# Self-attention of a decoder layer: the four key tiles' probabilities added on GpSimd, one product with ones per step

## Chip, cores and metric

The kernel runs on one core of a Trainium2 chip. The time is device microseconds of that core for one execution; three runs of the kernel before gave 2581.31 us as their median (2580.84 to 2584.7).

## What is computed

One decoder layer for B = 4 sequences of T = 512 rows with H = 512 features, in float32: a gated recurrence, a cross-attention over 1601 context rows, a causal self-attention with 16 heads of 32, and a mixture of experts with a shared expert. The change lies in the self-attention alone:

```python
q = (h @ wq + bq).reshape(B, S, N_HEADS, HEAD_DIM)   # k, v alike
q, k = _rope(q, k)
scores = jnp.einsum('bqhd,bkhd->bhqk', q, k) * HEAD_DIM ** (-0.5)
scores = jnp.where(causal[None, None], scores, jnp.finfo(scores.dtype).min)
attn = jax.nn.softmax(scores, axis=-1)
ctx = jnp.einsum('bhqk,bkhd->bqhd', attn, v).reshape(B, S, N_HEADS * HEAD_DIM)
x = x + ctx @ wo
```

## The kernel before

Four stages follow each other, each in a block of its own with a barrier behind it. Self-attention (`self_attention`) is the third and takes 16 **steps** (`STEPS`): step n works on sequence b = n // 4 and on the group c = n % 4 of four heads (`HPC` = 4). In a step the keys go by in four tiles of 128 rows, kt = 0 to 3. Because of the causal mask tile kt meets only the L = 512, 384, 256 or 128 queries behind it.

For a tile, TensorE (PE) computes the scores of the four heads into four PSUM banks (`scores`, L1727, the masks in L1731 and L1733); ScalarE (ACT) takes their exponential from all four banks in one instruction (L1529) into `pT`, a tile with two halves that alternate by kt; and `weighted` multiplies the probabilities by the values (L1745, into `o_bank`) and by a matrix of ones (L1747, into `sum_bank`). The second product gives the denominators of the softmax. The four heads of a product lie in four column groups of 32 of the array, so they run beside each other.

The maximum that softmax subtracts is made one step ahead. Between the scores of step n and those of its next key tile, PE writes plain scores for step n+1 into the *same four banks* (`maxima`, L1717 and L1719), and VectorE (DVE) reduces them (L1616) before PE may write the next scores there. At the end of a step PE transposes the four maxima (item T, L1711), ACT negates them (L1501), and they enter the next step's scores as one more product. Then DVE forms 1/sum from `sum_bank` (`reciprocal`, L1648), multiplies `o_bank` by it (L1650) and, with ACT (L1507), splits the result into a high and a low part (L1620) for the output projection.

PE's order is written out by hand in class `Steps`. A tile runs: scores(n, kt); the *early* items; maxima(n+1, 3-kt); weighted(n, kt); the *late* items. Items are the projections of later steps (A: queries and keys of step n+2; V: values; O: output projection of the sequence before; each 12 matmuls in L134), transposes of the next sequence's input (H, late in tiles 1 and 2 of c = 1, for b < 3), and in steps 14 and 15 the start of the experts (G, R, L). Step 1 has no item in tile 3, step 2 none in tiles 2 and 3, step 13 none in tile 2.

GpSimd (POOL) makes the rotary part of the queries and keys of step n+2 while step n runs: `rotate` (L1427 multiplies by cos, L1430 adds the part that DVE has turned in L1581 and multiplied by sin in L1583), then the high parts (L1444) and low parts (L1447), which wait until the scores of step n are done because the buffers alternate. It also makes inverse roots of four numbers (`inverse_root`, L1420), for H when c = 0 and for O when c = 3.

Of the kernel before, what the change touches and what calls it, by code (L numbers as in the profile page):

```python
# [20 lines left out]
P = 128  # L21
# [1301 lines left out]
def self_attention(nc, X, regions, first, ahead, hx, slots, ident, ident16, d):  # L1323
# [6 lines left out]
    with ExitStack() as stack:  # L1330
# [12 lines left out]
        qk = m.sb("qk", [P, 2, T])  # L1343
        turned = m.sb("turned", [P, 2, T])
        rot = m.sb("rot", [P, 2, T])
        pT = A.tile("s_pT", 0, 2, HPC, T)
        a_hi, a_lo = (A.tile(f"s_a{i}", (2 * HPC + i * RING) * T, RING, T, dt=F32R) for i in range(2))
        xs = A.tile("s_xs", (2 * HPC + 2 * RING) * T, TT, H)
        wo_raw = pT[:, 0]
        a = m.sb("a", [P, T])  # L1350
        topx = m.sb("topx", [P, TT, P])
        negm = m.sb("negm", [P, T], F32R)
# [4 lines left out]
        ss = m.sb("ss", [P, TT])  # L1357
        ms = m.sb("ms", [P, TT])
        rr = m.sb("rr", [P, TT])
        unused = pT[:, 1, :, T - P:T]  # L1360
        psum, bank = m.banks()
        s_apart = m.sem("apart")
        s_bank, o_bank, sum_bank = bank[0:HPC], bank[4], bank[5]
# [4 lines left out]
        s_whi, s_wlo = m.sem("whi", "wlo")  # L1368
        s_ss, s_ms, s_r, s_xs, s_put, s_hhi, s_hlo = m.sem("ss", "ms", "r", "xs", "put", "hhi", "hlo")
        s_vs, s_qb, s_tc, s_turned, s_sin, s_rot, s_hi, s_lo = m.sem("vs", "qb", "tc", "turned", "sin", "rot", "hi", "lo")  # L1370
        s_max, s_top, s_ng, s_st, s_ex, s_pv = m.sem("max", "top", "ng", "st", "ex", "pv")
        s_rec, s_a, s_ahi, s_alo, s_x1, s_x = m.sem("rec", "a", "ahi", "alo", "x1", "x")
        s_in, s_ahead, s_wrhi, s_wr = m.sem("in0", "in1"), m.sem("ahead"), m.sem("wrhi"), m.sem("wr")
        s_ghi, s_glo, s_lt, s_lc = m.sem("ghi", "glo", "lt", "lc")
# [32 lines left out]
        @block.gpsimd  # L1407
        def _(pool):
            pool.memset(half[:], -0.5).then_inc(s_const, 1)
            pool.memset(neg[:], 0.0).then_inc(s_const, 1)  # L1410
            pool.wait_ge(s_const, 2)
            pool.affine_select(out=neg[:], in_=neg[:], compare_op=ALU.is_ge, fill=-1e30, base=0,
                               pattern=[[-1, P]], channel_multiplier=1).then_inc(s_const, 1)

            def inverse_root(kind, b):
                u = line.root(kind, b)
                pool.wait_ge(s_ms, u + 1)
                if u:
                    pool.wait_ge(s_xs, u * TT)
                pool.tensor_tensor(rr[:], ms[:], half[:], ALU.pow).then_inc(s_r, 1)  # L1420

            def rotate(n, i):
                r = 2 * (n - 1) + i
                pool.wait_ge(s_qb, r + 1)
                if r >= 2:
                    pool.wait_ge(s_lo, r - 1)
                pool.tensor_tensor(rot[:, i], qk[:, i], cos[:], ALU.mult).then_inc(s_tc, 1)  # L1427
                pool.wait_ge(s_tc, r + 1)
                pool.wait_ge(s_sin, r + 1)
                pool.tensor_tensor(rot[:, i], rot[:, i], turned[:, i], ALU.add).then_inc(s_rot, 1)  # L1430

            pool.wait_ge(s_ld, 80)
            for n in range(1, STEPS):
                for i in range(2):
                    rotate(n, i)
                if n % KC == 2 and n // KC + 1 < B:
                    inverse_root("H", n // KC + 1)
                if n % KC == 1 and n // KC >= 2:
                    inverse_root("O", n // KC - 2)
                if n >= 2:  # L1440
                    pool.wait_ge(s_st, KC * (n - 1))
                for i in range(2):
                    pool.wait_ge(s_rot, 2 * (n - 1) + i + 1)
                    pool.tensor_copy(qk_hi[:, n % 2, i], rot[:, i]).then_inc(s_hi, 1)  # L1444
                for i in range(2):
                    pool.wait_ge(s_hi, 2 * (n - 1) + i + 1)
                    pool.tensor_tensor(qk_lo[:, n % 2, i], rot[:, i], qk_hi[:, n % 2, i], ALU.subtract).then_inc(s_lo, 1)  # L1447
            for b in (B - 2, B - 1):
                inverse_root("O", b)

        @block.scalar
        def _(act):
# [64 lines left out]
            for n in range(STEPS):  # L1517
                b, c = divmod(n, KC)
                if n == STEPS - 2:
                    act.wait_ge(s_ahead, 64)  # L1520
                    act.activation(wr_hi, wr, ACT.Copy).then_inc(s_wrhi, 1)
                for kt in range(TT):
                    L = T - kt * P
                    act.wait_ge(s_st, n * KC + kt + 1)
                    if n * TT + kt >= 2:
                        act.wait_ge(s_pv, n * TT + kt - 1)
                    else:
                        act.wait_ge(s_wlo, 1)
                    act.activation(pT[:, kt % 2, :, 0:L], psum[:, 0:HPC, 0:L], ACT.Exp, scale=SCALE).then_inc(s_ex, 1)  # L1529
                    if c == 1 and kt < 2 and b + 1 < B:  # L1530
                        normalise("H", b + 1, (2 * kt, 2 * kt + 1))
                    for item in line.early[n][kt]:
                        take(item)
                    if kt == 0 and n:
                        high_output(n - 1)
                    for item in line.late[n][kt]:
                        take(item)
                    if c == 0 and kt < 2 and b + 1 < B:
                        squares("H", b + 1, (2 * kt, 2 * kt + 1))
                    if c == 2 and kt == 0 and b:  # L1540
                        squares("O", b - 1, (0, 1))
                    if c == 3 and kt == 0 and b:
                        squares("O", b - 1, (2, 3))
                    if c == 3 and kt >= 2 and b:
                        normalise("O", b - 1, (2 * kt - 4, 2 * kt - 3))
                if n + 1 < STEPS:
                    take(line.turn[n + 1])
# [9 lines left out]
        def _(dve):  # L1557
# [71 lines left out]
            for n in range(STEPS):  # L1629
                b, c = divmod(n, KC)  # L1630
                if n == STEPS - 2:
                    dve.wait_ge(s_wrhi, 1)
                    dve.tensor_tensor(wr_lo, wr, wr_hi, ALU.subtract).then_inc(s_wr, 1)
                for kt in range(TT):
                    if n + 1 < STEPS:
                        maximum(n + 1, TT - 1 - kt)
                    if kt == 0 and n:
                        low_output(n - 1)
                    for item in line.early[n][kt] + line.late[n][kt]:
                        take(item)  # L1640
                    if c == 0 and kt == 2 and b + 1 < B:
                        mean("H", b + 1)
                    if c == 3 and kt == 0 and b:
                        mean("O", b - 1)
                dve.wait_ge(s_pv, n * TT + TT)
                if n:
                    dve.wait_ge(s_alo, n)
                dve.reciprocal(a[:], sum_bank).then_inc(s_rec, 1)  # L1648
                dve.wait_ge(s_rec, n + 1)
                dve.tensor_tensor(a[:], o_bank, a[:], ALU.mult).then_inc(s_a, 1)  # L1650
# [8 lines left out]
        def _(pe):  # L1659
# [76 lines left out]
            def weighted(n, kt):  # L1736
                c, L, qs = n % KC, T - kt * P, slice(kt * P, T)
                pe.wait_ge(s_ex, n * TT + kt + 1)
                if kt == 0 and n:
                    pe.wait_ge(s_a, n)  # L1740
                if n % KC == 0:
                    pe.wait_ge(s_vs, n // KC * TT + kt + 1)
                for j in range(HPC):
                    hd = c * HPC + j
                    pe.matmul(o_bank[rows[j], qs], v[:, kt, hd * SD:(hd + 1) * SD], pT[:, kt % 2, j, 0:L], start=kt == 0, stop=True, skip_group_check=True)  # L1745
                for j in range(HPC):
                    mm = pe.matmul(sum_bank[rows[j], qs], ones[:], pT[:, kt % 2, j, 0:L], start=kt == 0, stop=True, skip_group_check=True)  # L1747
                mm.then_inc(s_pv, 1)

            for t in reversed(range(TT)):  # L1750
                if t < TT - 1:
# [4 lines left out]
            for n in range(STEPS):  # L1756
                more = n + 1 < STEPS
                for kt in range(TT):
                    if kt == 0:
                        if n:  # L1760
                            pe.wait_ge(s_lo, 2 * n)
                    elif more:
                        pe.wait_ge(s_top, (n + 1) * TT + kt)
                    else:
                        pe.wait_ge(s_ex, n * TT + kt)
                    scores(n, kt)
                    for item in line.early[n][kt]:
                        put(item)
                    if more:
                        if kt == 0:  # L1770
                            pe.wait_ge(s_hi, 2 * n + 2)
                        pe.wait_ge(s_ex, n * TT + kt + 1)
                        maxima(n + 1, TT - 1 - kt)
                    weighted(n, kt)
                    for item in line.late[n][kt]:
                        put(item)
                if more:
                    put(line.turn[n + 1])
            for item in line.ahead + line.last + line.between + line.behind + line.end:
# [717 lines left out]
```

## Time and profile before

| | |
|---|---|
| runs of the kernel before, median | 2581.31 us |
| the profiled execution, its own time | 2578.19 us |
| its span in the profile | 2576.5 us |
| PE busy over the span | 2404.2 us, 93% |
| DVE busy | 1359.1 us, 53% |
| ACT busy | 1348.2 us, 52% |
| POOL busy | 908.1 us, 35% |
| granted TensorE clock, mean | 0.977 of full |

Start and end of the execution outside the span take 1.7 us. Busy time of PE is the time in which some matmul is under way, so the space between the starts of two groups of instructions tells more of what a product costs than its mean duration. In a timeline a row is a start (us from the start of the span), a duration, the engine, the line, the operation, out<-in, and in brackets the idle time of that engine just before it with what ended it. Self-attention's first exponential starts at 1416.3 us and its last step ends near 1827 us.

### The profile page before, as it was taken

Reading aid. Unit: us, or ns where it says so; the run is one execution under the profiler, and the core shown is the slowest. Engines: PE = TensorE matmul, PEld = TensorE weight load, DVE = VectorE, ACT = ScalarE, POOL = GpSimd, SP = SyncE. Lnnn points to the kernel's source line nnn. Section 1 sums busy time; section 2 is a strip of 40 time slices with the busy share of each in tenths; the row PEclk is TensorE's granted clock in tenths of the full one; section 3 lists DMA queues with packets and bytes.
Section 4 is the critical chain, followed back from the end, with each engine's and each line's share of the span. In section 5 each row is a group of like instructions: output and inputs, shape, how many; then the busy total and the mean of one; then the engine's idle time right before and its main releaser. Section 6 shows DMA issues by size and latency. Waiting matters only on the chain. (4 is left out here: it accounts for less than half of the span.)

```text
span 2576.5 us, 39055 instructions
## 1 busy us (share of the span) xinstructions
PE 2404.2 (93%) x15376; PEld 1549.9 (60%) x15376; DVE 1359.1 (53%) x2114; ACT 1348.2 (52%) x1708; POOL 908.1 (35%) x592
## 2 busy tenths in 40 slices
PE   6997899999999999999997999998799999999897
PEld 5885644444444444444333555565578899999786
DVE  5566634434344434434413556565565577776775
ACT  4221457667776777767895433443422266665221
POOL 1223744655355644555202333332031022221220
PEclk8998899999999999999998999999999999999999
DMA  5002685476547653665653200001153267775330
GB/s 179 17 1 76 190 219 125 120 205 164 150 111 211 169 150 98 184 184 140 178 115 119 95 1 1 17 18 52 62 171 131 87 222 244 243 239 194 108 123 33
DMA packets 208006, 331.45 MB, mean 129 GB/s; under 512 B 71312, under 2 KB 125840, under 8 KB 207632
## 3 DMA queue, kind: packets, MB, share of 16 engines
q1 hardware_dynamic: 190608, 256.99, 35.1%
q0 software_dynamic: 15056, 68.03, 8.1%
q10 hardware_dynamic: 2160, 3.93, 0.5%
q8 instruction: 122, 2.00, 0.3%
q14 instruction: 60, 0.49, 0.1%
HBM read 241.53 MB, written 99.42 MB: 132 GB/s over the span
## 5 line engine op out<-in xcount | busy, mean ns | idle before, releaser
L938 ACT ACTIVATE A_c_prob<-c_psum 128x1024 f32<-128x1024 f32 x832 | 787.0, 1030 | 291.3 <-PE c_psum L1188 284.6
L864 POOL TENSOR_TENSOR c_rr<-c_ms,c_half 128x32 f32<-128x32 f32 (+1 forms) x72 | 372.5, 5176 | 436.2 <-DVE c_ms L955 436.2
L1197 PE MATMUL c_psum<-A_c_prob,c_vq 128*17 128x512 f32 x3328 | 418.2, 603 | 11.1 <-DVE c_oT L1092 9.4
L134 PE MATMUL c_psum<-R_c_w,S_c_c 128*128 128x512 f32 x1248 | 314.3, 402 | 1.1 <-DVE S_c_c L966 0.5
L1188 PE MATMUL c_psum<-c_qq,c_kq 64*128 64x512 f32 x1664 | 290.4, 441 | 20.7 <-ACT A_c_prob L938 11.2
L134 PEld LDWEIGHTS c_psum<-R_c_w,S_c_c 128*128 128x128 f32 x1248 | 228.4, 189 | 123.4 <-issue 43.0
L1188 PEld LDWEIGHTS c_psum<-c_qq,c_kq 64*128 64x128 f32 x1664 | 138.1, 187 | 171.0 <-ACT A_c_prob L938 91.8
L2366 PE MATMUL m_psum<-A_m_dn_hi,A_m_a 128*128 128x512 f32 (+1 forms) x628 | 207.3, 399 | 10.6 <-DVE A_m_a L2170 10.6
L995 DVE COPY Q_c_unit<-c_psum 128x256 f32<-128x256 f32 x89 | 37.8, 425 | 333.5 <-PE c_psum L134 333.5
L134 PE MATMUL m_psum<-R_m_t,m_up_hi 128*128 128x256 f32 (+1 forms) x1104 | 200.0, 283 | 0.0
L1616 DVE TENSOR_REDUCE s_topx<-s_psum 128x4 f32<-128x2048 f32 (+1 forms) x64 | 95.5, 1492 | 172.8 <-PE s_psum L1719 170.0
L1197 PEld LDWEIGHTS c_psum<-A_c_prob,c_vq 128*17 128x17 f32 x3328 | 68.8, 96 | 191.6 <-issue 166.4
L134 PEld LDWEIGHTS m_psum<-R_m_t,m_up_hi 128*128 128x128 f32 (+1 forms) x1104 | 165.9, 180 | 2.1
L2109 ACT ACTIVATE A_m_a<-Q_m_work 128x256 fp32r<-128x256 f32 (+2 forms) x113 | 56.7, 502 | 209.9 <-DVE Q_m_work L2165 209.9
L134 PE MATMUL m_psum<-R_m_t,m_up_lo 128*128 128x256 f32 (+1 forms) x552 | 154.8, 280 | 0.0
L1529 ACT ACTIVATE A_s_pT<-s_psum 128x2048 f32<-128x2048 f32 (+1 forms) x64 | 79.4, 1240 | 125.4 <-PE s_psum L1733 125.1
L2366 PEld LDWEIGHTS m_psum<-A_m_dn_hi,A_m_a 128*128 128x128 f32 (+1 forms) x628 | 119.8, 191 | 38.1 <-DVE A_m_a L2170 11.9
L2102 ACT ACTIVATE Q_m_work<-m_psum 128x256 f32<-128x256 f32 (+2 forms) x113 | 51.8, 458 | 141.1 <-PE m_psum L134 141.1
L2366 PE MATMUL m_psum<-Q_m_dn_lo,A_m_a 128*128 128x512 f32 (+1 forms) x314 | 124.8, 397 | 0.0
L857 POOL TENSOR_TENSOR S_c_c<-Q_c_raw,S_c_c 128x512 fp32r<-128x512 f32 x89 | 119.4, 1341 | 7.1
L2022 POOL DMA_INDIRECT S_up_raw<-in_up,m_up_row x46 | 43.5, 947 | 196.5 <-DVE m_up_lo L2147 196.5
L134 PE MATMUL m_psum<-R_g_hi,m_up_hi 128*128 128x512 f32 x264 | 105.5, 400 | 3.6 <-DVE m_up_lo L2147 3.6
(296 smaller groups left out, 4329.8 us busy)
## 6 DMA issues: line engine op xcount, KB each, us to landing
c_kq<-kd SPq DMA_DIRECT2D x248, 208.0 KB, 5.9
kd<-S_c_t SPq DMA_DIRECT2D x96, 256.0 KB, 3.4
Q_c_raw<-in_ctxT SPq DMA_DIRECT2D x89, 256.0 KB, 4.9
qd<-A_c_q SPq DMA_DIRECT2D x64, 256.0 KB
c_qq<-qd SPq DMA_DIRECT2D x64, 256.0 KB, 3.2
vd<-A_c_vt SPq DMA_DIRECT2D x104, 136.0 KB, 3.2
c_vq<-vd SPq DMA_DIRECT2D x31, 442.0 KB, 9.3
R_m_hs<-slots SPq DMA_DIRECT2D x23, 512.0 KB, 8.2
```

What stands on the lines that cost most here:

```text
L134: mm = pe.matmul(out, a(c), b(c), start=first and i == 0, stop=last and i == len(terms) - 1)
L857: pool.tensor_tensor(c_lo[:, job % 2], c_raw[:, n % CB], c_hi[:, job % 2], ALU.subtract).then_inc(s_clo, 1)
L864: pool.tensor_tensor(rr[:, unit % RB, 0:n], ms[:, unit % RB, 0:n], half[:, 0:n], ALU.pow).then_inc(s_r, 1)
L938: act.activation(prob[:, t % PB, 2 * (u % 2):2 * (u % 2) + 2, :], score_banks[u % 3], ACT.Exp, scale=XD ** -0.5).then_inc(s_ex, 1)
L1188: mm = pe.matmul(score_banks[u % 3][:, s, :], kq[rows, q % 2, u % 2, kt * P:(kt + 1) * P], qq[rows, q % 2, u % 2, :], start=True, stop=True)
L1197: mm = pe.matmul(o_bank[32 * j:32 * j + VW, :], vq[:, q % 2, kt, j, :], prob[:, t % PB, j, :], start=kt == 0, stop=kt == CT - 1)
L1529: act.activation(pT[:, kt % 2, :, 0:L], psum[:, 0:HPC, 0:L], ACT.Exp, scale=SCALE).then_inc(s_ex, 1)
L1616: dve.reduce_max(topx[:, t, ::SD], psum[:, 0:HPC, 0:(t + 1) * P], AX_X).then_inc(s_top, 1)
L2022: pool.indirect_dma_start(up_raw[:, j].rearrange("p k n -> p (k n)"), None, d["up"], bass.IndirectOffsetOnAxis(up_row[:, j, tile:tile + 1] ...
L2102: act.activation(sig[0:rows, 0:width], gu_bank[n % 2][0][0:rows, 0:width], ACT.Sigmoid).then_inc(s_sig, 1)
L2109: act.activation(a_hi[0:rows, p % 2, i, 0:width], act_f[0:rows, 0:width], ACT.Copy).then_inc(s_ahi, 1)
L2366: mm = pe.matmul(y_bank[t], a[0:rows, p % 2, i, ts], w[0:rows, i, :], start=k == 0, stop=k == 3 * len(x.chunks) - 1)
```

## The change

The two halves of `pT` become `p_even`, which keeps tile 0's probabilities for the whole step, and `p_odd`, in which tiles 1, 2 and 3 follow each other. On POOL the new `add(n, kt)` adds tile kt (kt = 1, 2, 3) of all four heads into the matching columns of tile 0: 4 x 384, 4 x 256 and 4 x 128 elements in each partition. `weighted` keeps only the product with the values. A new `sums(n)` at the end of the step's tiles waits for the third addition and multiplies the total by ones, once, for all 512 queries; T of the next step comes behind it. The exponential of tile 2 or 3 now waits for the addition of the tile before it (same buffer), that of the next step's tile 0 for `sums`, and the reciprocal for `sums` too. On POOL the loop is turned: add 1; the O root (c = 3); rotate of q; add 2; rotate of k; add 3; the H root (c = 0); high and low parts.

```diff
-        pT = A.tile("s_pT", 0, 2, HPC, T)
+        p_even, p_odd = (A.tile(f"s_p{i}", i * HPC * T, HPC, T) for i in range(2))
+        pT = [p_even, p_odd[:, :, 0:T - P], p_odd[:, :, 0:T - 2 * P], p_odd[:, :, 0:P]]
...
+            def add(n, kt):
+                pool.wait_ge(s_pv, n * TT + 1)
+                pool.wait_ge(s_ex, n * TT + kt + 1)
+                if kt > 1:
+                    pool.wait_ge(s_add, n * (TT - 1) + kt - 1)
+                pool.tensor_tensor(pT[0][:, :, kt * P:T], pT[0][:, :, kt * P:T], pT[kt], ALU.add).then_inc(s_add, 1)
+
+            pool.wait_ge(s_ld, 80)
+            for i in range(2):
+                rotate(1, i)
+            halves(1)
+            for n in range(STEPS):
+                b, c = divmod(n, KC)
+                more = n + 2 < STEPS
+                add(n, 1)
+                if c == KC - 1 and b:
+                    inverse_root("O", b - 1)
+                if more:
+                    rotate(n + 2, 0)
+                add(n, 2)
+                if more:
+                    rotate(n + 2, 1)
+                add(n, 3)
+                if c == 0 and b + 1 < B:
+                    inverse_root("H", b + 1)
+                if more:
+                    halves(n + 2)
+            inverse_root("O", B - 1)
...
-                    if n * TT + kt >= 2:
-                        act.wait_ge(s_pv, n * TT + kt - 1)
-                    else:
+                    if kt == 0 and n:
+                        act.wait_ge(s_sum, n)
+                    if kt == 0 and n == 0:
                         act.wait_ge(s_wlo, 1)
-                    act.activation(pT[:, kt % 2, :, 0:L], psum[:, 0:HPC, 0:L], ACT.Exp, scale=SCALE).then_inc(s_ex, 1)
+                    if kt >= 2:
+                        act.wait_ge(s_pv, n * TT + kt)
+                        act.wait_ge(s_add, n * (TT - 1) + kt - 1)
+                    act.activation(pT[kt], psum[:, 0:HPC, 0:L], ACT.Exp, scale=SCALE).then_inc(s_ex, 1)
...
-                dve.wait_ge(s_pv, n * TT + TT)
+                dve.wait_ge(s_sum, n + 1)
...
+                    mm = pe.matmul(o_bank[rows[j], qs], v[:, kt, hd * SD:(hd + 1) * SD], pT[kt][:, j, :], start=kt == 0, stop=True, skip_group_check=True)
+                mm.then_inc(s_pv, 1)
+
+            def sums(n):
+                pe.wait_ge(s_add, (n + 1) * (TT - 1))
                 for j in range(HPC):
-                    mm = pe.matmul(sum_bank[rows[j], qs], ones[:], pT[:, kt % 2, j, 0:L], start=kt == 0, stop=True, skip_group_check=True)
-                mm.then_inc(s_pv, 1)
+                    mm = pe.matmul(sum_bank[rows[j], :], ones[:], pT[0][:, j, :], start=True, stop=True)
+                mm.then_inc(s_sum, 1)
...
                     for item in line.late[n][kt]:
                         put(item)
+                sums(n)
                 if more:
                     put(line.turn[n + 1])
```

## Rows read from the trace of the kernel before

**Rows 1.** Step 11: us; busy PE, PEld, DVE, ACT, POOL; PEclk, DMA share, GB/s.
```profile
1701.50:1727.40 25.90, 24.32 (x232) 15.55 (x232) 14.64 (x16) 12.51 (x18) 9.79 (x9) 1.00 0.06 22
```
**Rows 2.** Waits, 1410 to 1850 us: who waited for whom, total us, times, longest.
```profile
PEld s_psum L1727 <- DVE s_topx L1616: 43.9, 38, 1.5
```
**Rows 3.** Timeline of PE, step 11: tile 0, then the step's end.
```profile
1706.52 1.06 PE L1745 MATMUL s_psum<-A_s_pT,s_v 128*32 128x512 f32 x8
1707.40 1.04 PE L1747 MATMUL s_psum<-A_s_pT,s_ones 128*32 128x512 f32 x8
1708.97 0.45 PE L1727 MATMUL s_psum<-Q_s_qk 32*128 32x384 f32 x4 [0.53 <-DVE s_topx L1616]
...
1726.10 0.40 PE L1747 MATMUL s_psum<-A_s_pT,s_ones 128*32 128x128 f32 x8
1726.80 0.63 PE L1711 MATMUL s_psum<-ident,s_topx 128*128 128x128 f32 x4 [0.30 <-DVE s_topx L1616]
```
**Rows 4.** Timeline of DVE, step 11: reductions, the product with sin, the reciprocal.
```profile
1706.63 2.29 DVE L1616 TENSOR_REDUCE s_topx<-s_psum 128x4 f32<-128x2048 f32 x1 [0.60 <-PE s_psum L1719]
...
1716.28 0.69 DVE L1583 TENSOR_TENSOR s_turned<-s_turned,s_sin 128x512 f32<-128x512 f32 x1
...
1725.96 0.69 DVE L1616 TENSOR_REDUCE s_topx<-s_psum 128x4 f32<-128x512 f32 x1 [4.50 <-PE s_psum L1719]
1726.57 3.35 DVE L1648 RECIPROCAL s_a<-s_psum 128x512 f32<-128x512 f32 x1
```
**Rows 5.** Timeline of ACT, step 11: the exponentials of tiles 1, 2 and 3.
```profile
1710.32 1.46 ACT L1529 ACTIVATE A_s_pT<-s_psum 128x1536 f32<-128x1536 f32 x1 [1.80 <-PE s_psum L1733]
...
1716.77 1.03 ACT L1529 ACTIVATE A_s_pT<-s_psum 128x1024 f32<-128x1024 f32 x1 [2.96 <-PE s_psum L1733]
...
1722.55 0.60 ACT L1529 ACTIVATE A_s_pT<-s_psum 128x512 f32<-128x512 f32 x1 [1.15 <-PE s_psum L1733]
```
**Rows 6.** Instruction groups of POOL by shape, whole span: busy us, mean ns.
```profile
L1430 POOL TENSOR_TENSOR s_rot<-s_rot,s_turned 128x512 f32<-128x512 f32 x30 | 38.6, 1286 | 69.9 <-DVE s_turned L1583 69.9
...
L1444 POOL CAST Q_s_qk<-s_rot 128x512 fp32r<-128x512 f32 x30 | 17.5, 611 | 36.3 <-PE s_psum L1733 36.3
L1420 POOL TENSOR_TENSOR s_rr<-s_ms,s_half 128x4 f32<-128x4 f32 x7 | 7.1, 1017 | 68.1 <-DVE s_ms L1570 68.1
...
L883 POOL CAST R_s_hi<-A_c_stage 128x2048 fp32r<-128x2048 f32 x2 | 3.8, 1898 | 12.8 <-DMA A_c_stage<-in_wq 12.1 <-DMA A_c_stage<-in_wv 0.7
```
**Rows 7.** Timelines of POOL and DVE before step 0: two instructions that meet.
```profile
1411.46 4.59 POOL L1447 TENSOR_TENSOR Q_s_qk<-s_rot,Q_s_qk 128x512 fp32r<-128x512 f32 x2
...
1412.08 2.82 DVE L1628 TENSOR_TENSOR s_w_lo<-A_s_pT,s_w_hi 128x2048 fp32r<-128x2048 f32 x1
```
**Rows 8.** Timeline of PE, end of step 0.
```profile
1439.51 0.43 PE L1747 MATMUL s_psum<-A_s_pT,s_ones 128*32 128x128 f32 x8
1439.99 0.63 PE L1711 MATMUL s_psum<-ident,s_topx 128*128 128x128 f32 x4
```
**Rows 9.** Timelines of PE and DVE, step 1 (H transposes late in tiles 1 and 2).
```profile
1455.31 0.39 PE L1727 MATMUL s_psum<-Q_s_qk 32*128 32x256 f32 x4
...
1463.39 0.63 PE L1711 MATMUL s_psum<-ident,s_topx 128*128 128x128 f32 x4 [0.30 <-DVE s_topx L1616]
...
1452.97 1.76 DVE L1616 TENSOR_REDUCE s_topx<-s_psum 128x4 f32<-128x1536 f32 x1 [2.88 <-PE s_psum L1719]
```
**Rows 10.** Timelines of ACT and PE, step 2 (no item in tiles 2 and 3).
```profile
1472.87 1.46 ACT L1529 ACTIVATE A_s_pT<-s_psum 128x1536 f32<-128x1536 f32 x1 [3.16 <-PE s_psum L1733]
...
1485.64 0.63 PE L1711 MATMUL s_psum<-ident,s_topx 128*128 128x128 f32 x4 [0.30 <-DVE s_topx L1616]
```
**Rows 11.** Timeline of PE, step 13, tile 2, where matmuls ran slower.
```profile
1771.18 1.10 PE L1747 MATMUL s_psum<-A_s_pT,s_ones 128*32 128x256 f32 x8
```
**Rows 12.** Timelines of ACT and DVE, step 15, the last.
```profile
1817.84 1.45 ACT L1529 ACTIVATE A_s_pT<-s_psum 128x1536 f32<-128x1536 f32 x1 [0.16 <-PE s_psum L1733]
...
1827.97 3.36 DVE L1648 RECIPROCAL s_a<-s_psum 128x512 f32<-128x512 f32 x1 [0.82 <-PE s_psum L1747]
```

More of the change, by code:

```diff
@@ L1345, in self_attention @@
         rot = m.sb("rot", [P, 2, T])
-        pT = A.tile("s_pT", 0, 2, HPC, T)
+        p_even, p_odd = (A.tile(f"s_p{i}", i * HPC * T, HPC, T) for i in range(2))
+        pT = [p_even, p_odd[:, :, 0:T - P], p_odd[:, :, 0:T - 2 * P], p_odd[:, :, 0:P]]
         a_hi, a_lo = (A.tile(f"s_a{i}", (2 * HPC + i * RING) * T, RING, T, dt=F32R) for i in range(2))
         xs = A.tile("s_xs", (2 * HPC + 2 * RING) * T, TT, H)
-        wo_raw = pT[:, 0]
+        wo_raw = pT[0]
         a = m.sb("a", [P, T])
@@ L1359, in self_attention @@
         rr = m.sb("rr", [P, TT])
-        unused = pT[:, 1, :, T - P:T]
+        unused = p_odd[:, :, T - P:T]
         psum, bank = m.banks()
@@ L1370, in self_attention @@
         s_vs, s_qb, s_tc, s_turned, s_sin, s_rot, s_hi, s_lo = m.sem("vs", "qb", "tc", "turned", "sin", "rot", "hi", "lo")
-        s_max, s_top, s_ng, s_st, s_ex, s_pv = m.sem("max", "top", "ng", "st", "ex", "pv")
+        s_max, s_top, s_ng, s_st, s_ex, s_pv, s_add, s_sum = m.sem("max", "top", "ng", "st", "ex", "pv", "add", "sum")
         s_rec, s_a, s_ahi, s_alo, s_x1, s_x = m.sem("rec", "a", "ahi", "alo", "x1", "x")
@@ L1430, in rotate, with halves @@
                 pool.tensor_tensor(rot[:, i], rot[:, i], turned[:, i], ALU.add).then_inc(s_rot, 1)
[L1432 to L1439, printed above, removed]
+            def halves(n):
                 if n >= 2:
@@ L1447, in _ @@
                     pool.tensor_tensor(qk_lo[:, n % 2, i], rot[:, i], qk_hi[:, n % 2, i], ALU.subtract).then_inc(s_lo, 1)
-            for b in (B - 2, B - 1):
-                inverse_root("O", b)
+            def add(n, kt):
[25 more added lines that the diff above has]
+            inverse_root("O", B - 1)
         @block.scalar
@@ L1744, in weighted @@
                     hd = c * HPC + j
-                    pe.matmul(o_bank[rows[j], qs], v[:, kt, hd * SD:(hd + 1) * SD], pT[:, kt % 2, j, 0:L], start=kt == 0, stop=True, skip_group_check=True)
+                    mm = pe.matmul(o_bank[rows[j], qs], v[:, kt, hd * SD:(hd + 1) * SD], pT[kt][:, j, :], start=kt == 0, stop=True, skip_group_check=True)
+                mm.then_inc(s_pv, 1)
+            def sums(n):
+                pe.wait_ge(s_add, (n + 1) * (TT - 1))
                 for j in range(HPC):
-                    mm = pe.matmul(sum_bank[rows[j], qs], ones[:], pT[:, kt % 2, j, 0:L], start=kt == 0, stop=True, skip_group_check=True)
-                mm.then_inc(s_pv, 1)
+                    mm = pe.matmul(sum_bank[rows[j], :], ones[:], pT[0][:, j, :], start=True, stop=True)
+                mm.then_inc(s_sum, 1)
             for t in reversed(range(TT)):
```

## The prediction, made before the changed kernel was run

> **What bounds the kernel now.** I read the windows of single steps first, then the waits, then the timelines of PE, DVE, ACT and POOL over one step. In step 11 PE is busy 24.32 of 25.90 us [rows 1], so self-attention looks PE-bound, and taking matmuls from it looks like pure gain. The waits say otherwise: the scores (L1727) waited for the reduction of the maxima 38 times, on their weight loads 43.9 us in all [rows 2]. The timeline shows why. Scores of this step and maxima of the next use the same banks, so each tile ends in a serial piece: maxima, reduction on DVE, next scores. In tile 0 the reduction runs 1706.63 to 1708.92 [rows 4] and the next scores start at 1708.97 [rows 3]; the products with values and ones from 1706.52 on lie beside it, and PE is still idle for 0.53 us. The products that the change removes mostly fill time in which PE must wait.
>
> **Removed.** The product with ones takes 0.88 us of PE for 512 queries, taken as equal to the product with the values beside it (1707.40 less 1706.52 [rows 3]). By columns that is 0.66, 0.44 and 0.22 for tiles 1 to 3: 2.20 a step. One product of 0.88 stays, so 1.32 a step goes, 21 us in 16 steps, if PE's order alone counted. But in tiles 0 to 2 of an ordinary step the next scores wait for DVE, and only PE's idle time grows: worth 0.
>
> **The step's end.** Before, the transposes T start at 1726.80, 0.15 after the last reduction ends (1725.96 + 0.69) [rows 3, 4]; the tile-3 product with ones began at 1726.10. Now a product of 512 begins there. It takes 0.88, and about 0.1 more until what follows it starts (an estimate: the x8 groups last 1.04 to 1.06 where the starts are 0.88 apart [rows 3]). T comes at 1727.08: **+0.28** where reduction 3 releases T, in steps 3, 6, 7, 10 and 11: +1.4. Where a V item in tile 3 delays the weighted product (c = 0), ones begin at 1439.51 and T at 1439.99 [rows 8]; T moves to 1440.49: +0.5 in steps 0, 4, 8, 12: +2.0. In steps 5, 9, 13, 14 the T transposes wait for the DVE work on an O item, which hides the new product. The reciprocal (1726.57 [rows 4]) now starts about 0.1 after T. DVE stays free in time: before it had 0.60 idle ahead of the tile-0 reduction [rows 4].
>
> **Added on POOL.** No row has a float32 addition of 1536 elements. One of 512 takes 1.29 us (L1430). Casts of 512 and 2048 take 0.61 and 1.90, so 0.18 of a cast is fixed; with 0.18 fixed, the additions take 3.49, 2.39 and 1.29 us [rows 6]. Upper bound, all proportional: 3.86, 2.57, 1.29. Lower bound: as much fixed as the 1.02 of L1420 on four elements: 1.82, 1.55, 1.29. I take the middle ones, since casts are nearest in kind.
>
> **The lock.** Before step 0 DVE's two-input L1628 (2048 elements) and POOL's L1447 meet. Two L1447 take 4.59 us instead of 2.58 and end at 1416.05; DVE's takes 2.82 from 1412.08, which is until 1414.90 [rows 7]. That fits DVE waiting until POOL's first ends near 1412.7, then POOL's second standing until DVE ends (1414.90 + 1.29 = 1416.19). So I let such a pair exclude each other for a whole instruction; reductions and reciprocals, which read PSUM, do not take part. The Trainium skill states this too ("SBUF — State Buffer", Who interferes with whom: a DVE instruction with two SBUF inputs contends with a GpSimd one that reads SBUF, and the loser fully blocks); this trace agrees. Without the rule POOL's chain would be 0.6 shorter in each step with a k item in tile 1 and the sum about 1.2 us lower.
>
> **The POOL chain.** Time zero is the end of tile 1's exponential, 1711.77 [rows 5]. Addition 1: 0.07 to 3.56; tile 2's exponential, which now waits for it, is wanted at 5.00 (1716.77). Rotation q is 2.57; L1583 is wanted at 4.51 (1716.28 [rows 4]), waits for POOL's first multiplication to end at 4.85 and holds POOL for 0.6: 6.7. Addition 2 to 9.1; tile 3's exponential is wanted at 10.78. Rotation k to 11.7; tile 3's exponential ends at 11.38; addition 3 to 13.0. `sums` is wanted at 14.33. With the O root (1.02, steps 7 and 11) it is 14.0, still in time. The additions hide in ordinary steps, with 1.3 and 0.3 us to spare. Then the high and low parts: 2 x 0.61 + 2 x 1.29 [rows 6], to about 17; the next maxima, which end at the tile-0 reduction's start, want the high parts near 20 (1706.63 + 25.9 less 0.9 for themselves [rows 1, 4]). Addition 2 or 3 shows where a step has no items:
> - **Step 1**: H transposes come late in tiles 1 and 2, and there PE is the bound: the scores start at 1455.31, the reduction had ended at 1454.73 [rows 9]. Removing 0.66 and 0.44 gives 0.53 + 0.5, cut only by DVE. But tile 3 has no item. Tile 1's exponential ends at 1450.9; addition 1 to 54.5, rotation with lock 57.7, addition 2 60.1, rotation 62.7, addition 3 63.9, `sums` 64.0, T 65.0 against 1463.39: **+1.6**.
> - **Step 2**: tile 1's exponential ends 1474.33; 77.9, 81.1, 83.5, 86.1, 87.4, `sums` 87.5, T 88.4 against 1485.64 [rows 10]: **+2.8**.
> - **Steps 5, 9**: as step 1, but two O items cover the additions: **-1.0** each. **Step 14**: R stands late in tile 2, -0.5. **Step 13**: PE ran slower in this profile, four heads' 256 columns from 1771.18 taking 1.10 [rows 11], where twice the columns take 1.04 [rows 3], and PE was the bound of that tile: -0.4.
> - **Step 15**: there are no maxima. The exponential of tile 1 ends 1819.3; addition 1 to 22.8, exponential 23.9, the root meanwhile, addition 2 26.3, exponential 27.0, addition 3 28.3, `sums` 28.4 to 29.3, reciprocal at 29.5 against 1827.97 [rows 12]: **+1.5**. The output projection hangs on it, and a barrier ends the stage, so it is passed on in full.
>
> **Sum**: 1.4 + 2.0 + 1.6 + 2.8 - 2.0 - 0.5 - 0.4 + 1.5 = **+6.4 us**. With the lower POOL bound steps 1, 2, 15 give 0, 1.2, 0.2: +1.9. With the upper: 2.1, 3.3, 2.0 and 0.3 each in steps 7 and 11: +8.5. The profiled execution took 2578.19 us, so 2584.6 by its clock; the median of the runs shown is 3.1 higher, and against it the forecast is **2587.7 us**.
>
> **Rivals.**
> 1. *PE is the bound after all* (faster). If DVE's reductions ended before PE wanted its banks, 1.32 a step would count from the first step on: 21 us, 2560. For it: PE's 94% in the window. Against: 38 waits at exactly this place. It decides at a tile-0 reduction of 1.8 us; it takes 2.29. Chance 0.07.
> 2. *POOL is slower than its 512 row says*. The additions walk four pieces of 384, 256 and 128 elements, no row does. At 4.5, 3.0 and 1.5 us rotation q with lock ends at 7.75, addition 2 at 10.75, rotation k 13.3, addition 3 14.8: every ordinary step loses 0.5, those with the root 1.5, steps 1, 2, 15 1.8 more each, some 10 us on top: 2598. It needs an addition 1 over 4.1 us. Chance 0.11.
> 3. *The clock falls more often.* In step 13 matmuls ran at about half speed, the lower of the two levels, for some 3.5 us after PE had stood waiting for the exponential. The change lengthens the waits in every tile, and steps 1 and 2 come to pauses of 2.5 us. Three more such falls at 1.7 us each give 2593. Against it: one fall in 16 steps so far. The Trainium skill ("TensorE: Matmul & The Clock Gate", HAM oscillation) holds that pauses between bursts bring the clock down; the trace bears it out only in step 13. Chance 0.11.
> 4. *Nothing reaches the end*: the gains of steps 5, 9, 13, 14 and small slacks cancel the losses, within 3 us of before, about 2583. Chance 0.09.
>
> **Numbers.** The forecast has the remaining 0.62. A measurement of this kernel tells some 0.2% from no change, 5.2 us. Of the forecast's band (+1.9 to +8.5, centre 6.4) 0.34 lies beyond 5.2 and 0.28 within; with rivals 2 and 3 slower is 0.56, with rival 4 same is 0.37, faster 0.07. The range leaves out rival 1 and what lies beyond rival 2: 2578 to 2598; its foot is the lower POOL bound less the runs' spread and a step 1 or 2 better than worked out.
>
> **What would show it.** Right: PE's busy share in step 11 falls to some 23 of 26.2 us, yet the step is no shorter; PE's idle time before L1727 grows to 1.4, 1.1 and 0.75 us; T stands 0.98 behind the start of `sums`; POOL is busy some 17 us a step; additions of 3.5, 2.4 and 1.3; L1583 of tile 1 near 1.0. Steps 1, 2 and 15 carry most of the loss, and there PE waits for POOL. Wrong: steps under 25.5 us (rival 1), POOL as the releaser of ACT's L1529 or of `sums` in ordinary steps (rival 2), PEclk under 1 in several steps (rival 3).

## The result, and the profile after

The changed kernel takes 2592.63 us, the median of five runs (2590.8 to 2596.64), beside 2581.31 us for five runs of the kernel before. The ratio is 1.0042, with a 95% interval of 1.0028 to 1.0057: slower by some 11 us. Once more, in a later series: 2593.72 beside 2582.96, ratio 1.0048 (1.0034 to 1.0062). The forecast was 2587.7, slower by 6.4 us, in a range of 2578 to 2598. The direction and the range held; the size was 0.6 of what came.

The head of the page of the changed kernel, the engines' busy time over the whole span:

```profile
span 2589.7 us, 38367 instructions
...
PE 2392.3 (92%) x14992; PEld 1543.0 (60%) x14992; DVE 1362.3 (53%) x2114; ACT 1349.1 (52%) x1708; POOL 1022.7 (39%) x640
```

PE is busy 12 us less and does 384 matmuls fewer; POOL is busy 115 us more; the span is 13 us longer. An ordinary step of the new kernel (step 11, columns as in [rows 1]), by the windows view:

```profile
1707.40:1733.60 26.20, 22.99 (x208) 14.78 (x208) 14.11 (x16) 12.51 (x18) 16.03 (x12) 1.00 0.07 25
```

PE was busy 24.32 of 25.90 us there [rows 1]; now 22.99 of 26.20. The matmuls went, and the step is 0.3 us longer. PE's timeline of the same step, tile 0 and the end of the step:

```profile
1712.42 1.06 PE L1769 MATMUL s_psum<-A_s_p,s_v 128*32 128x512 f32 x8
1714.88 0.45 PE L1751 MATMUL s_psum<-Q_s_qk 32*128 32x384 f32 x4 [1.39 <-DVE s_topx L1640]
...
1731.98 1.04 PE L1775 MATMUL s_psum<-A_s_p,s_ones 128*32 128x512 f32 x8
1732.95 0.66 PE L1735 MATMUL s_psum<-ident,s_topx 128*128 128x128 f32 x4
```

This answers to [rows 3]. The next scores start 2.46 us after the product with the values, as they did before (1706.52 to 1708.97: 2.45); PE's idle time before them grew from 0.53 to 1.39, by just what was taken out. In tiles 1 and 2 it is 1.07 and 0.75; the forecast had 1.4, 1.1 and 0.75. At the end T starts 0.97 after the product with ones, where it stood 0.70 after the smaller one. The waits view of self-attention:

```profile
PEld s_psum L1751 <- DVE s_topx L1640: 70.0, 41, 2.3
...
PEld s_psum L1775 <- POOL A_s_p L1448: 4.4, 3, 1.9
ACT A_s_p L1553 <- POOL A_s_p L1448: 3.9, 2, 2.6
```

The wait for the reduction went from 43.9 us [rows 2] to 70.0; it swallowed the saving. The additions hold up PE at `sums` in three places and the exponential in two.

The starts of the transposes T give every step's length. A table of their distances in the traces, in us; the last column runs from T of step 15 to the first matmul of the experts:

| kernel | 0 | 1 | 2 | 3 | 4 | 5 | 11 | 13 | 14 | 15, end | all |
|---|---|---|---|---|---|---|---|---|---|---|---|
| before | 25.91 | 23.40 | 22.25 | 25.94 | 25.92 | 29.80 | 25.94 | 29.47 | 28.28 | 50.20 | 446.6 |
| changed | 26.48 | 25.49 | 27.11 | 28.01 | 26.47 | 28.92 | 26.22 | 30.74 | 27.80 | 55.40 | 463.2 |
| forecast of the difference | +0.5 | +1.6 | +2.8 | +0.28 | +0.5 | -1.0 | +0.28 | -0.4 | -0.5 | +1.5 | +6.4 |
| measured difference | +0.57 | +2.09 | +4.86 | +2.07 | +0.55 | -0.88 | +0.28 | +1.27 | -0.48 | +5.20 | +16.6 |

(Step 9 goes like 5, 8 and 12 like 4, 6, 7 and 10 like 11.) Eleven of the 16 places came out within 0.15 us of the forecast. The others are steps 1, 2 with 3, 13 and the end. This trace has 16.6 us more in the stage than the trace before, and so has a second trace of the changed kernel, while the runs differ by 11. Part of the gap lies outside the stage: the first T stands at 1410.18 us, before at 1414.08, and over the twelve traces of this case it lies anywhere from 1408.4 to 1418.4, whatever the kernel. How much the stage grew in the runs that have no trace is not known. POOL's timeline in step 2, with DVE's multiplication by sin and PE's end of the step:

```profile
1474.88 3.45 POOL L1448 TENSOR_TENSOR A_s_p<-A_s_p,A_s_p 128x1536 f32<-128x1536 f32 x1 [11.09 <-ACT A_s_p L1553]
1478.29 1.29 POOL L1428 TENSOR_TENSOR s_rot<-s_qk,s_cos 128x512 f32<-128x512 f32 x1
1479.65 1.59 POOL L1431 TENSOR_TENSOR s_rot<-s_rot,s_turned 128x512 f32<-128x512 f32 x1
1481.21 2.35 POOL L1448 TENSOR_TENSOR A_s_p<-A_s_p,A_s_p 128x1024 f32<-128x1024 f32 x1
1483.52 1.26 POOL L1428 TENSOR_TENSOR s_rot<-s_qk,s_cos 128x512 f32<-128x512 f32 x1
1484.86 1.27 POOL L1431 TENSOR_TENSOR s_rot<-s_rot,s_turned 128x512 f32<-128x512 f32 x1
1486.08 1.26 POOL L1448 TENSOR_TENSOR A_s_p<-A_s_p,A_s_p 128x512 f32<-128x512 f32 x1
...
1479.28 0.84 DVE L1607 TENSOR_TENSOR s_turned<-s_turned,s_sin 128x512 f32<-128x512 f32 x1
...
1487.40 1.93 PE L1775 MATMUL s_psum<-A_s_p,s_ones 128*32 128x512 f32 x8 [0.76 <-POOL A_s_p L1448]
```

POOL works without a gap from the first addition on: 12.5 us in which two rotations stand between three additions, as worked out. But the product with ones takes 1.93 us where step 11's takes 1.04: the clock. The windows view over the stretches where it was down (PEclk is the third number from the end):

```profile
1458.00:1466.00 8.00, 6.32 (x45) 3.13 (x44) 4.38 (x3) 0.75 (x2) 5.79 (x6) 0.57 0.01 2
1482.00:1494.00 12.00, 9.81 (x77) 5.49 (x73) 5.55 (x4) 2.23 (x3) 8.82 (x8) 0.57 0.00 0
1776.00:1784.00 8.00, 7.24 (x46) 5.08 (x47) 1.23 (x1) 1.00 (x2) 7.92 (x7) 0.57 0.22 76
1834.00:1842.00 8.00, 6.13 (x32) 3.63 (x32) 4.03 (x2) 4.25 (x7) 1.27 (x1) 0.57 0.21 78
1844.00:1850.00 6.00, 6.00 (x20) 4.72 (x20) 3.61 (x6) 0.72 (x2) 0.00 (x0) 0.72 0.00 0
1862.00:1865.00 3.00, 2.83 (x14) 2.86 (x15) 0.88 (x2) 1.40 (x3) 0.00 (x0) 0.50 0.61 227
```

Six falls to the lower level, 0.5 of full, stand in the changed kernel's trace between step 1 and the end: in step 1, in step 2 (reaching into step 3), in step 13, and three behind T of step 15. Before there was one in that stretch, in step 13 [rows 11]; one more begins in either trace some 1.1 to 1.5 us before the experts' first matmul. The runs without a trace bear it out: the mean granted clock of the 11 runs of the changed kernel lies between 0.971 and 0.974, 0.972 on average, that of the runs of the kernel before at 0.976 on average.

The fall in step 2 does not come from the pause at `sums`. It is there before that pause begins: the product of the same step's last 128 queries, from 1485.99, already takes 0.66 us, where the one at full clock in step 1 (from 1458.17) takes 0.43. In step 1 the clock falls inside the pause, which lasts 1.68 us. The last step, by the timelines of ACT and DVE, which answer to [rows 12]:

```profile
1830.26 1.03 ACT L1553 ACTIVATE A_s_p<-s_psum 128x1024 f32<-128x1024 f32 x1 [2.61 <-POOL A_s_p L1448]
...
1837.94 3.36 DVE L1672 RECIPROCAL s_a<-s_psum 128x512 f32<-128x512 f32 x1 [4.45 <-PE s_psum L1775]
```

The reciprocal stands 20.0 us after T, before 17.5: +2.5, of which 0.9 is the slow product with ones. Another 2.7 us come behind it, where stretches at the lower clock lie; that these cost just 2.7 is not shown.

### The profile page after: what moved, and what is told of

Read it like the earlier page. It is cut to its first block and busy times, and to the rows that moved or that the text cites. A ratio compares the mean times of both kernels' runs of the same rounds, so it can differ in the third digit from the quotient of the medians.

```text
span 2589.7 us, 38367 instructions
## 1 busy us (share of the span) xinstructions
PE 2392.3 (92%) x14992; PEld 1543.0 (60%) x14992; DVE 1362.3 (53%) x2114; ACT 1349.1 (52%) x1708; POOL 1022.7 (39%) x640
## 5 line engine op out<-in xcount | busy, mean ns | idle before, releaser
L1448 POOL TENSOR_TENSOR A_s_p<-A_s_p,A_s_p 128x1536 f32<-128x1536 f32 (+2 forms) x48 | 113.8, 2370 | 172.5 <-ACT A_s_p L1553 172.4
L1553 ACT ACTIVATE A_s_p<-s_psum 128x2048 f32<-128x2048 f32 (+1 forms) x64 | 79.4, 1240 | 127.5 <-PE s_psum L1757 123.3
```

The lines of the kernel that those rows point to most:

```text
L1448: pool.tensor_tensor(pT[0][:, :, kt * P:T], pT[0][:, :, kt * P:T], pT[kt], ALU.add).then_inc(s_add, 1)
L1553: act.activation(pT[kt], psum[:, 0:HPC, 0:L], ACT.Exp, scale=SCALE).then_inc(s_ex, 1)
```

## The experiments

Ten series of runs follow, of eight further kernels, one of them twice, and of the changed kernel again, each beside runs of the kernel before on the same chip. Theory A is the forecast's: POOL's chain is exposed in steps 1, 2 and 15, the single product costs 0.3 to 0.5 us where nothing hides it, and falls of the clock come on top.

### The old products kept

```diff
+                for j in range(HPC):
+                    mm = pe.matmul(sum_bank[rows[j], qs], ones[:], pT[kt][:, j, :], start=kt == 0, stop=True, skip_group_check=True)
                 mm.then_inc(s_pv, 1)
```

> All of the change, and the old products with ones stay in each tile too; the last product overwrites what they wrote. Nothing that the change saves on PE is saved. Theory A (these products lie in PE's waits for the reduction): ordinary steps last the same as in the changed kernel to 0.05 us; steps 5 and 9 lose the 0.9 us they had gained, step 14 0.5; at most 3 us above the changed kernel, and fewer clock falls if idle PE causes them, then as fast or faster than it. Rival (PE is the bound): 2.2 us a step of work comes back, less nothing: 20 to 35 us above the changed kernel.

2594.63 us, ratio 1.0047 (1.003 to 1.0065): no slower than the changed kernel by anything that can be told (1.0042 and 1.0048). Step 11 of it, by the windows view:

```profile
1708.00:1734.40 26.40, 25.13 (x240) 15.79 (x236) 14.08 (x16) 12.52 (x18) 16.03 (x12) 1.00 0.06 21
```

PE does 2.14 us more in the step than in the changed kernel (25.13 for 22.99), and T to T is 26.43, 0.2 longer. The 0.2 was missed: I had said 0.05. It fits the kept product of tile 3 (0.22 us by columns), which now stands ahead of `sums` with nothing to hide it. The other three cost nothing in such a step. Steps 5 and 9 go back to 29.85 and 29.82, the kernel before's 29.80 and 29.84, as expected. So PE is not the bound in ordinary steps, and rival 1 is shown wrong.

The expectation also said that the clock would fall less if idle PE causes the falls. It did: in steps 1 to 3 this trace has one fall of some 3 us instead of two that last 17 together, the three steps are 24.87, 24.62 and 26.45 long where the changed kernel has 25.49, 27.11 and 28.01, and the mean clock of the nine runs is 0.975 instead of 0.972. So the equal time is the sum of two things: the kept products lose what steps 5, 9 and 14 had gained and 0.2 us in most others, and the clock gives about as much back.

### No additions

```diff
-                add(n, 1)
...
-                add(n, 2)
...
-                add(n, 3)
...
-                        act.wait_ge(s_add, n * (TT - 1) + kt - 1)
...
-                pe.wait_ge(s_add, (n + 1) * (TT - 1))
+                if n == 0:
+                    pe.wait_ge(s_ld, 80)
                 for j in range(HPC):
-                    mm = pe.matmul(sum_bank[rows[j], :], ones[:], pT[0][:, j, :], start=True, stop=True)
+                    mm = pe.matmul(sum_bank[rows[j], :], ones[:], cos[:], start=True, stop=True)
```

> The change without its additions on POOL and without the waits for them. The product with ones at a step's end runs over another tile of the same size (the cosine table), so the denominators are not those of the softmax. Theory A: POOL's exposed part is gone, what remains is +0.3 to +0.5 at the end of nine steps, -0.8 in step 1, -1 in steps 5 and 9, -0.5 in step 14, +0.5 at the end: 0 to +2 us against the kernel before, and no more clock falls than it if the falls need the long waits for POOL. Rival B (short waits in every tile bring the clock down): falls stay in steps 2, 13 and the end, +5 to +8 us. Rival D (additions slow everything, by the shared port too): well below before.

2585.94 us, ratio 1.002 (1.0006 to 1.0033), by the ratio some 5 us above the kernel before (by the medians 3.4), where Theory A had 0 to 2 and rival B 5 to 8. So half of the loss or more goes with the additions and their waits. Step 1 is 22.76 (-0.64, expected -0.8), the ordinary steps are as in the changed kernel (26.22, 26.46), step 14 27.80. But step 2 is 24.19 and step 3 27.17, 1.9 and 1.2 above before with no POOL in the way, and step 13 is 29.90, where before had 29.47 and the forecast 29.07: falls of the clock without the long pauses. The mean clock of the twelve runs is 0.974, between 0.976 before and 0.972. Here rival B was right.

### Additions first

```diff
                 add(n, 1)
...
-                if more:
-                    rotate(n + 2, 0)
                 add(n, 2)
-                if more:
-                    rotate(n + 2, 1)
                 add(n, 3)
+                if more:
+                    rotate(n + 2, 0)
+                    rotate(n + 2, 1)
```

> All of the change, but POOL makes the three additions of a step right behind their exponentials and both rotations after them. Theory A (the loss sits where POOL's chain is exposed: steps 1, 2 and the last; steps that end in the 512-column product lose 0.3 to 0.5; the clock falls came from the long pauses there): `sums` waits for POOL about 0.4 us in steps 1 and 2 instead of 2.4, no clock fall in steps 2 and 3, step 15 unchanged; in all 4 to 8 us under the changed kernel, +2 to +7 us against the kernel before. Rival B (PE's shorter waits in every tile bring the clock down, wherever POOL stands): falls remain, the time stays within 2 us of the changed kernel's +11. Rival C (the rotations come too late for the next maxima): PE's first instruction of the maxima waits for the high parts from POOL in most steps, 0.5 to 1 us each, slower than the changed kernel.

2588.99 us, ratio 1.0025 (1.001 to 1.004): +6.4, some 4 us under the changed kernel, as Theory A had it in time; but the falls in steps 2 and 3, which it said would go, stayed, as rival B had it. The wait of `sums` shrank: in step 1, 0.39 us, and T to T is 23.34, where the changed kernel has 25.49 and the one before 23.40. Rival C came in small: in step 2 the maxima wait 0.34 us for the high parts, and in no step over 0.8. PE's timeline in step 2:

```profile
1472.85 0.51 PE L1740 MATMUL s_psum<-Q_s_qk 32*128 32x512 f32 x4 [0.34 <-POOL Q_s_qk L1438]
...
1482.73 0.39 PE L1750 MATMUL s_psum<-Q_s_qk 32*128 32x256 f32 x4 [1.07 <-DVE s_topx L1639]
...
1484.92 0.58 PE L1740 MATMUL s_psum<-Q_s_qk 32*128 32x256 f32 x4 [1.11 <-ACT A_s_p L1552]
...
1485.98 1.08 PE L1768 MATMUL s_psum<-A_s_p,s_v 128*32 128x256 f32 x8
...
1491.11 1.94 PE L1774 MATMUL s_psum<-A_s_p,s_ones 128*32 128x512 f32 x8
```

The 256 columns from 1485.98 take 1.08 us, at full clock 0.64. The clock was still full from 1483 to 1484.2 us and fell in the second of two pauses, of 1.07 and 1.11 us, with 1.1 us of matmuls between them; neither pause had to do with POOL. And `sums` waits for nothing, yet takes 1.94. Step 2 is 25.46, 3.2 above before. The reorder cures the pause and not the fall.

### Spare products in the pauses

```diff
             def sums(n):
+                if n in (1, 2, 15):
+                    pe.wait_ge(s_ld, 80)
+                    for j in list(range(HPC)) * 2:
+                        pe.matmul(sum_bank[rows[j], :], ones[:], cos[:], start=True, stop=True)
                 pe.wait_ge(s_add, (n + 1) * (TT - 1))
```

> All of the change, and in steps 1, 2 and 15 PE makes two spare products of 512 columns (1.8 us, overwritten) between its last tile and `sums`, where it stands waiting for POOL's additions for 0.8 to 2.4 us. Theory A (POOL's chain is the price and the clock falls because PE stands idle in it): steps 2 and 3 get 2 to 3.5 us shorter in all than in the changed kernel's trace (27.11 and 28.01), though the spare products add up to 0.5 us where the wait is shorter than they are; in all 1 to 4 us under the changed kernel. Rival B (the falls come from PE's short waits in the tiles before, not from this pause): falls remain where they were, steps 1, 2 and 15 get longer by 0 to 1 us each, the changed kernel's time or up to 3 us more.

2593.7 us, ratio 1.0047 (1.0033 to 1.0061), the same as the changed kernel of that series (2593.72). In time this was a miss for Theory A. The trace is between the theories: step 1 is 24.67 (25.49 without the spare products), its clock full throughout, step 3 26.22 (28.01), the ordinary value; but step 2 is 26.84 (27.11), since the clock fell there before the spare products began. PE's timeline at the ends of steps 1 and 2:

```profile
1459.77 1.90 PE L1776 MATMUL s_psum<-s_cos,s_ones 128*32 128x512 f32 x16
1461.67 1.07 PE L1779 MATMUL s_psum<-A_s_p,s_ones 128*32 128x512 f32 x8
...
1485.44 3.28 PE L1776 MATMUL s_psum<-s_cos,s_ones 128*32 128x512 f32 x16
1488.55 1.03 PE L1779 MATMUL s_psum<-A_s_p,s_ones 128*32 128x512 f32 x8
```

In step 2 the spare products run mostly at the lower clock (3.28 us for what takes 1.90 in step 1) and the product after them at full clock again. With PE busy the clock is back earlier; what it gains is 2.8 us over the stage in this trace, less than six runs can tell. It is the rest of a gain and two losses: the spare products hold up `sums` where POOL is done before them. In step 2 `sums` starts 2.3 us after the last addition has ended, and in step 15 the reciprocal stands 21.34 us after T, where the changed kernel has 20.00.

### The steps apart

One kernel text, in which a tuple says which steps use additions and the single product; all others multiply each tile by ones as before (the waits, which change with it, are left out below). POOL's loop keeps the new order.

```diff
+        ADDED = (0, 3, 4, 5, 6, 7, 8, 9, 10, 11, 12, 13, 14)
+        prob = lambda n, kt: pT[kt] if n in ADDED else (p_even, p_odd)[kt % 2][:, :, 0:T - kt * P]
...
+                if n not in ADDED:
+                    for j in range(HPC):
+                        mm = pe.matmul(sum_bank[rows[j], qs], ones[:], prob(n, kt)[:, j, :], start=kt == 0, stop=True, skip_group_check=True)
                 mm.then_inc(s_pv, 1)
```

All but 1, 2 and 15:

> Additions and the single product in all steps but 1, 2 and 15, which multiply each tile by ones as before. Theory A: +0.55 in four steps, +0.28 in five, -0.9 in steps 5 and 9, -0.5 in step 14, 0 to -0.4 in step 13: about +1 us against the kernel before, and 8 to 10 us under the changed kernel. Rival E (the loss is spread over all steps by the shorter tiles and falls of the clock in them): +5 us or more against the kernel before.

2584.68 us, ratio 1.0006 (0.9995 to 1.0018). About +1.5 us, forecast +1; the mean clock of its twelve runs is 0.976 to 0.977, no lower than before. Its trace still has a fall at the end of step 2 that makes step 3 27.50 long. Then 1, 2 and 15 alone, `ADDED = (1, 2, 15)`:

> The complement: additions and the single product only in steps 1, 2 and 15. Theory A: +1.6, +2.8 and +1.5 us by the sum of the prediction, and the falls of the clock that their pauses bring, 2 us in steps 2 and 3 and 3 us at the end: +6 to +11 us against the kernel before, nearly the whole loss of the change. Rival E: +6 at most, the falls being in the other steps too.

2596.7 us, ratio 1.0052 (1.0035 to 1.0068), +13: three steps give the whole loss of sixteen, and the upper end of the expectation is passed a little. Steps 1, 2 and 3 are 25.47, 27.34 and 27.83, the end 56.34, and the mean clock of the six runs is 0.972. Step 10, which has no additions here, is 27.44 long instead of 25.98, with a fall in it. Rival E is out.

In no step, `ADDED = ()`:

> Additions in no step: the kernel before with POOL's loop turned as the change has it. Theory A: the turned loop alone costs nothing, every step as before to 0.1 us, 0 +- 2 us. Rival: the new order of rotations and roots is part of the loss, steps of 26.2 us instead of 25.9.

2581.82 us, ratio 1.0005 (0.9992 to 1.0019); steps 0 to 12 as before to 0.04 us. The turned loop costs nothing. The end of this trace is 53.81 instead of 50.20 us, though the code there does the same: the end of the stage varies by itself, and the 5.2 us that the changed kernel's trace shows there are not all of its making.

Only where the changed kernel was faster, `ADDED = (5, 9, 14)`, twice:

> Additions and the single product only in steps 5, 9 and 14, where the trace of the changed kernel shows a gain (T to T 0.88, 0.92 and 0.48 us shorter); the other thirteen steps multiply each tile by ones as before. POOL's loop keeps its new order. Theory A: 2.3 us under the kernel before, about 2579, at the edge of what can be measured; in the trace steps 5, 9, 14 as in the changed kernel and all others as before. Rival (the turned loop of POOL costs something by itself): other steps longer than before, no gain.

2579.75 us, ratio 0.9988 (0.9973 to 1.0002). Step 2 of this trace does what it did before and is yet 23.38 long instead of 22.25; the windows view shows a fall there:

```profile
1480.00:1486.00 6.00, 4.89 (x62) 2.81 (x63) 2.49 (x3) 1.02 (x1) 1.27 (x1) 0.72 0.00 0
```

> The kernel with additions in steps 5, 9 and 14 alone, once more, to narrow its ratio to the kernel before (0.9988, 0.9973 to 1.0002 so far). Theory A, from the traces: 2.3 us less than before, ratio 0.999. Rival: no difference, ratio 1.000.

2576.78 us beside 2581.11, ratio 0.9986 (0.9976 to 0.9996): faster than the kernel before by about 3.6 us, 0.14%. The forecast was 2.3; the steps that were changed gave 2.4 in the trace. Steps 5 and 9 are 28.86 each (29.80 and 29.84 before), step 14 27.80 (28.28), all other steps up to 12 within 0.05 of before.

### The changed kernel again

> The changed kernel once more, for its time beside the kernels of this series and for a second trace: which falls of the clock come again. Theory A: +9 to +13 us against the kernel before; falls of the clock in steps 2 or 3 and behind step 15 again. Rival (falls are chance): they lie in other steps.

2593.72 us, ratio 1.0048. Its steps repeat to 0.06 us everywhere: 25.51, 27.08, 27.97 for 1 to 3, 30.68 for 13, 55.42 at the end, with the falls in the same places. In this kernel their places are not chance.

## Why the prediction was right, and what was too small in it

**The bound.** "In tiles 0 to 2 of an ordinary step the next scores wait for DVE, and only PE's idle time grows: worth 0." Shown, by the timeline (2.46 for 2.45 us) and by the kept products.

**The step's end.** +0.28 and +0.5: measured +0.26 to +0.32 and +0.54 to +0.57. The product in the place of the smaller one takes 0.97 to T, estimate 0.98.

**The additions.** Taken as 3.49, 2.39 and 1.29 us, between bounds far apart. POOL's groups by shape:

```profile
L1448 POOL TENSOR_TENSOR A_s_p<-A_s_p,A_s_p 128x1536 f32<-128x1536 f32 x16 | 55.4, 3462 | 164.8 <-ACT A_s_p L1553 164.8
...
L1448 POOL TENSOR_TENSOR A_s_p<-A_s_p,A_s_p 128x1024 f32<-128x1024 f32 x16 | 37.9, 2366 | 1.7 <-ACT A_s_p L1553 1.7
...
L1448 POOL TENSOR_TENSOR A_s_p<-A_s_p,A_s_p 128x512 f32<-128x512 f32 x16 | 20.5, 1283 | 6.0 <-ACT A_s_p L1553 5.9
```

3.46, 2.37, 1.28: the fixed part read from two casts was right, and the four pieces of each row cost nothing. Rival 2 (an addition over 4.1 us) is out.

**The lock.** Right in kind, too large in size where POOL stood first. DVE's multiplication, 0.69 us alone [rows 4], took 0.84 in step 2 while POOL's multiplication ended, and POOL's next took 1.59 instead of 1.28: 0.3 us of delay, not 0.6, which makes the chain so much shorter than worked out. In step 11 DVE stood first at 1722.18 and POOL's multiplication from 1722.22 took 1.80, 0.5 more than alone. The Trainium skill ("SBUF — State Buffer", Who interferes with whom) says of the port pair that the two engines share that whoever issues first has it for the whole instruction and the other is blocked. The trace agrees in kind, in both orders; the delays that it shows, 0.3 and 0.5 us, are shorter than the 0.69 us of the whole instruction.

**The exposed steps.** Step 1 was to lose 1.6; it lost 1.27 with the clock up (spare products) and 2.09 with it down. Step 2 was to lose 2.8 and lost 4.86, with 1.8 more in step 3. What POOL's chain alone costs in step 2 is seen in the kernel that kept the old products, whose step 2 begins at full clock (T at 1464.62):

```profile
1475.70 3.47 POOL L1448 TENSOR_TENSOR A_s_p<-A_s_p,A_s_p 128x1536 f32<-128x1536 f32 x1 [8.52 <-ACT A_s_p L1553]
...
1488.24 1.07 PE L1777 MATMUL s_psum<-A_s_p,s_ones 128*32 128x512 f32 x8 [0.50 <-POOL A_s_p L1448]
```

The first addition starts 11.1 us after T, `sums` 23.6, and the step is 24.62 long: +2.4. In the changed kernel the same two stand at 12.7 and 25.3, since the fall of step 1 slows the beginning of step 2, and the product with ones takes 0.9 longer: 2.5 us of the 4.86 are the clock's. The places were right: three steps carry all of it.

**What was too small** is the clock. The sum behind "The forecast has the remaining 0.62" holds no term for new falls; the clock stands beside it as rival 3 at 0.11 instead of in it. Rival 3 said: three more falls at 1.7 us, 2593. That number was nearer, its sign (PEclk under 1 in several steps) came, and its mechanism ran together with the forecast's, not in its place. Taken at full clock, the steps lost +1.3 (1), +2.4 (2), +0.28 (3), +1.6 (15, up to the reciprocal) and in the others what the table shows: 6.6 us without step 13, where the forecast has 6.8. That leaves 10.0 of this trace's 16.6 us for the clock: 5.1 in steps 1 to 3, 1.3 in step 13 and 3.6 at the end. The last of these is not all the change's, since a kernel whose code there is as before also showed 3.6 more. Over the runs the loss is 11 to 12 us, so some 5 are left for the clock, by subtraction. An upper bound (an estimate from the mean clocks, 0.972 and 0.976): 0.004 of 2590 us, some 10 us.

Step 13 was worked out as -0.4 because the profile before had a fall there, and a PE at the lower clock is the bound and gains from the removal; in the new kernel the fall came again and lasted longer. Without a fall that step takes 28.24 us in the kernel with additions in no step; it is 1.2 longer in the trace before and 2.5 in the changed kernel's. What the change does to it at full clock no trace shows; its +1.27 is counted to the clock here.

**Luck.** The band that the forecast gave its own sum, +1.9 to +8.5, is 2583 to 2590 us, and the result lies above it. The range held because its top was set by rival 2, slow additions, which did not come.

**What stays open** is what exactly sets off a fall. Falls came without POOL's pauses too (no additions, additions first), and in places where nothing was changed: step 13 of the kernel before, the end of the kernel with additions in no step, step 2 of one of two traces with additions in 5, 9 and 14, step 10 with additions in 1, 2 and 15. In both traces of the changed kernel they came in the same places. Filling the long pause removed the fall in step 1 and kept the one in step 2 from reaching into step 3. The mean clock of the runs says where the additional ones belong: 0.972 for the changed kernel and for the one that has additions in steps 1, 2 and 15 alone, 0.976 or a little more before and with additions everywhere but there, 0.974 with no additions or with the additions first, 0.975 with the old products kept. So it is the less filled PE of those three steps that brings more falls; a condition for a single fall was not found.

## What to carry to other kernels

Before work is taken off the busiest engine, look at what ends each of its waits: work that lies beside a wait is free, and taking it out only lengthens the wait. A chain moved to an idle engine is priced in the places with the least work around it, not in the ordinary step; and where a change only works in some steps, use it in those: three of sixteen gave 0.14%, all sixteen lost 0.4 to 0.5%. An engine left more idle can also run slower: make the clock a term of the sum.

## What was not expected of the hardware

In step 2 PE's clock fell to its lower level though no pause before it in that step was longer than 1.4 us: in the additions-first kernel in the second of two pauses of 1.07 and 1.11 us with 1.1 us of matmuls between, and it stayed down for 8 us and more (0.50 from 1486 to 1494). A group of 512-column products then took 1.94 us instead of 1.04. The changed kernel's falls came again at the same places in its second trace.
